# Two layers of a residual graph network on one core: row sums kept by left and right half, turned on VectorE in 32x32 blocks instead of on TensorE, tile columns in row order

## The reference

```
x = layernorm(x + adj @ (x * (u >= 0.1) / 0.9))          # layer 1
x = layernorm(x + adj @ (x @ weight) + bias)             # layer 2
```

## Time and profile before

| | us |
|---|---|
| median of 3 runs | 902.74 (902.63 to 902.84) |
| the profiled execution | 902.77 |
| its span | 901.0 |
| TensorE busy | 873.1 |
| VectorE busy | 529.6 |
| mean granted TensorE clock | 0.997 |

### The profile page before, as it was taken

One profiled execution on the slowest core, in us unless ns is written; L12 is line 12 of the kernel. 1 busy time (PEld: TensorE's weight loads), 2 busy tenths in 40 slices (PEclk: granted clock), 3 DMA queues, 4 the chain that ended last, 5 costly groups with the idle time before them and its releaser, 6 DMA issues.

```text
span 901.0 us, 13601 instructions
## 1 busy us (share of the span) xinstructions
PE 873.1 (97%) x5754; PEld 406.1 (45%) x5754; DVE 529.6 (59%) x1026; ACT 30.2 (3%) x74; POOL 25.3 (3%) x24
## 2 busy tenths in 40 slices
PE   3899999999999999999999999999999999999996
PEld 3653333333343444535354554636446456456343
DVE  6356123126145656766676667768677768768655
ACT  0100000000000000000000000000000000000011
POOL 3000000000000000000000000000000000000133
PEclk9999999999999999999999999999999999999998
DMA  9999999999999999999999999989899999999952
GB/s 373 411 416 421 420 420 420 421 421 420 420 420 422 419 420 420 420 401 410 420 420 403 413 404 380 422 352 422 359 408 419 414 417 419 420 421 419 420 242 71
DMA packets 55404, 359.60 MB, mean 399 GB/s; under 512 B 6448, under 2 KB 10544, under 8 KB 12592
## 3 DMA queue, kind: packets, MB, share of 16 engines
q1 hardware_dynamic: 55344, 358.74, 96.7%
HBM read 356.61 MB, written 2.10 MB: 398 GB/s over the span
## 4 chain that ended last, share of the span: by engine, by line
PE 92%; DMA 4%; SPq 2%; issue 1%; DVE 1%; POOLq 0%; POOL 0%; ACT 0%; DVEq 0%
PE psum L996 22%; PE psum L949 21%; PE psum L964 8%; PE psum L931 8%; PE psum L958 8%; PE psum L982 6%; PE psum L917 5%; PE psum L938 4%; PE psum L1002 4%; DMA tiles<-adj_chunks 2%; DMA tiles<-adj_t 2%; PE psum L894 1%; SPq L495 1%; PE psum L1017 1%; PE psum L1032 1%
## 5 line engine op out<-in xcount | busy, mean ns | idle before, releaser
L949 PE MATMUL psum<-tiles,stat 128*64 128x512 f32 x976 | 216.8, 593 | 0.1
L996 PE MATMUL psum<-tiles,stat 128*64 128x512 f32 x944 | 211.7, 594 | 0.0
L656 DVE TENSOR_TENSOR layer<-psum,layer 128x512 f32<-128x512 f32 (+1 forms) x143 | 98.6, 689 | 182.8 <-PE psum L996 85.6
L949 PEld LDWEIGHTS psum<-tiles,stat 128*64 128x64 f32 x976 | 69.6, 137 | 128.2 <-issue 122.5
L996 PEld LDWEIGHTS psum<-tiles,stat 128*64 128x64 f32 x944 | 66.5, 137 | 123.7 <-issue 121.4
L692 DVE TENSOR_TENSOR tiles<-tiles 128x512 f32<-128x512 f32 x90 | 62.2, 691 | 53.7 <-PE psum L940 51.7
L966 PE MATMUL psum<-tiles,stat 128*64 128x256 f32 x360 | 92.7, 380 | 0.0
L933 PE MATMUL psum<-tiles,stat 128*64 128x256 f32 x360 | 92.4, 379 | 0.0
L931 PE MATMUL psum<-tiles,stat 128*64 128x256 f32 x360 | 92.4, 379 | 0.0
L931 PEld LDWEIGHTS psum<-tiles,stat 128*64 128x64 f32 x360 | 49.3, 137 | 40.9 <-issue 20.0
L680 DVE TENSOR_TENSOR tiles<-tiles 128x512 f32<-128x512 f32 x90 | 60.6, 683 | 10.0 <-DMA tiles<-adj_t 10.0
(11 more groups left out here) (100 smaller groups left out, 849.5 us busy)
## 6 DMA issues: line engine op xcount, KB each, us to landing
tiles<-adj_t SPq DMA_DIRECT2D x306, 1024.0 KB, 13.4
tiles<-adj SPq DMA_DIRECT2D x12, 1024.0 KB, 19.2
tiles<-adj_chunks SPq DMA_DIRECT2D x12, 1024.0 KB, 20.4
tiles<-xu SPq DMA_DIRECT2D x4, 1024.0 KB, 7.9
tiles<-adj_parts SPq DMA_DIRECT2D x16, 256.0 KB, 17.7
x_res<-x SPq DMA_DIRECT2D x16, 128.0 KB, 13.9
out<-layer SPq DMA_DIRECT2D x8, 256.0 KB, 2.1
w<-weight SPq DMA_DIRECT2D x4, 16.0 KB, 9.6
```

Of the source, the lines that this page charges most:

```text
L656: return dve.tensor_tensor(out=to, in0=addend, in1=to, op=ALU.add)
L949: last = pe.matmul(sum_f[i % 2][to, :], stat[:, j * C + c, 0:D], tile[:, c], start=begun.get("f") != i and c < 2, stop=ends and c >= 2, sk ...
L996: last = pe.matmul(bank[to, :], stat[:, j * C + c, D:2 * D], tile[:, c], start=c == 0, stop=c == C - 1)
```

## The change

The sums of a row are kept differently. For each chunk c the left 256 columns of the tile are summed in PSUM partitions 0 to 63 and the right 256 in partitions 64 to 127, so every sum is complete where it stands: 8 matmuls of 256 columns in place of 4 of 512. The four transposes on TensorE and the copies on ScalarE are gone. At `row_end` VectorE adds the layer 1 part by halves, transposes 128x256 in 32x32 blocks from `halves` (row 1: straight from PSUM) to PSUM, and adds x in eight operations of 32 partitions and 128 elements each, some of them from one group of 32 partitions to another. Then it normalises as before, all of it without a filler between. `centre_weights` comes behind the norm of row 14. The part turns of block row 0 keep their transposes on TensorE.

The host now puts the columns of a tile in the order of the rows, 4p + c. So `final` reads its stationary operand with a step of 4 elements (16 bytes). Block row 0 in its first four tiles is stored by parts, and `arrived` gives them out with the part as the innermost axis: neighbouring columns lie 512 elements (2 KiB) apart there. Only `pair(0, 0)` to `pair(0, 3)` read them so.

```diff
@@ order_of_work
-            if pieces and (i > 1 or len(filler) % 2 == 0):
+            if pieces and (len(filler) == ECHO_BANKS if i > 1 else len(filler) % 2 == 0):
...
             if not turned:
                 turned = True
-                jobs.append(("turn", i - 1) if i > 1 else ("part_turn", PARTS - 1))
+                if i == 1:
+                    jobs.append(("part_turn", PARTS - 1))
...
@@ vector engine, in place of turn(k, i, c)
+            def turn(i):
+                k = turns(i) - 1
+                dve.wait_ge(s_res[i % 2], 16 * (i // 2 + 1))
+                dve.wait_ge(h_ready, k)
+                source = sum_f[i % 2] if i < EARLY else halves
+                last = dve.transpose(turned[:, 0:B // 2], source[:, 0:B // 2].rearrange("f (e p c) -> f e c p", e=2, c=C))
...
+                for side in range(2):
+                    for features in range(2):
+                        for e in range(2):
+                            at = slice((2 * side + features) * QUAD, (2 * side + features + 1) * QUAD)
+                            to = slice((2 * side + e) * QUAD, (2 * side + e + 1) * QUAD)
+                            f = slice(features * QUAD, (features + 1) * QUAD)
+                            last = dve.scalar_tensor_tensor(out=r[to, :, f], in0=t[at, e], scalar=KEPT, in1=x_rows[to, :, f],
+                                                            op0=ALU.mult, op1=ALU.add)
...
+                normalise(i, slice(0, C))
+                if EARLY <= i < NB - 2:
+                    sum_stat(i)
+                if i == NB - 2:
+                    centre_weights()
@@ vector engine, row_end
-                    dve.wait_ge(turned_ready, turns(i - 1))
                     dve.wait_ge(tile_jobs_done, done_after[job])
...
-                        dve.tensor_tensor(out=halves[of_row(i), :], in0=sum_f[i % 2][of_row(i), :],
-                                          in1=layer1_pair(i)[of_row(i), :], op=ALU.add).then_inc(half_by_dve, 1)
...
+                        own = layer1_pair(i)[of_row(i), :]
+                        step(dve.tensor_tensor(out=halves[0:D, 0:B // 2], in0=sum_f[i % 2][0:D, 0:B // 2],
+                                               in1=own[:, 0:B // 2], op=ALU.add))
+                        dve.tensor_tensor(out=halves[D:P, 0:B // 2], in0=sum_f[i % 2][D:P, 0:B // 2],
+                                          in1=own[:, B // 2:B], op=ALU.add).then_inc(half_by_dve, 1)
+                        dve.wait_ge(half_by_dve, turns(i))
+                    turn(i)
@@ tensor engine
-                    return tiles[:, slot].rearrange("p q (c b) -> p c q b", c=C)
+                    return tiles[:, slot].rearrange("p q (c b) -> p c b q", c=C)
...
                         for c in range(C):
-                            to = low if c % 2 == 0 else high
-                            last = pe.matmul(sum_f[i % 2][to, :], stat[:, j * C + c, 0:D], tile[:, c],
-                                             start=begun.get("f") != i and c < 2, stop=ends and c >= 2,
-                                             skip_group_check=True)
+                            for to, columns in (low, left), (high, right):
+                                last = pe.matmul(sum_f[i % 2][to, left], stat[:, j * C + c, 0:D], tile[:, c, columns],
+                                                 start=begun.get("f") != i and c == 0, stop=ends and c == C - 1,
+                                                 skip_group_check=True)
...
-                    for c in range(C):
-                        last = pe.transpose(turned[:, c * P:(c + 1) * P], halves[:, c * P:(c + 1) * P], ident[:, :])
-                    last.then_inc(turned_ready, 1)
...
-                            last = pe.matmul(product[n_final % 2][:, to], layer2[at, i // 2, c * P:(c + 1) * P],
+                            last = pe.matmul(product[n_final % 2][:, to], layer2[at, i // 2].rearrange("f (p c) -> f c p", c=C)[:, c],
                                              w2[at, :], start=True, stop=True)
@@ host
-    a = np.asarray(adj).reshape(NB, P, C, NB, P, C).transpose(0, 3, 4, 5, 2, 1)
+    a = np.asarray(adj).reshape(NB, P, C, NB, P, C).transpose(0, 3, 4, 5, 1, 2)
```

More of the change, by code:

```diff
@@ L34 @@
 C = 4
+QUAD = 32
 B = C * P
@@ L239, in order_of_work @@
         jobs.append(("row_end", i))
-    jobs += again[:1]
-    jobs.append(("turn", NB - 1))
-    jobs += again[1:]
+    jobs += again
     pending = None
@@ L319, in resnorm_graph_layers @@
     for job in jobs:
-        if job[0] in ("row_end", "turn"):
+        if job[0] == "row_end":
             chain_at = done_after[job]
@@ L555, in _ @@
                 elif job[0] == "row_end":
-                    i = job[1]
-                    act.wait_ge(turned_ready, turns(i - 1))
-                    act.wait_ge(tile_jobs_done, done_after[job])
-                    other = slice(D, P) if i >= EARLY and i % 2 == 0 else slice(0, D)
-                    act.activation(halves[other, :], sum_f[i % 2][other, :], ACT.Copy).then_inc(half_by_act, 1)
-                elif job[0] == "turn":
                     act.wait_ge(centred, turns(job[1]))
@@ L729, in combine, with normalise @@
                 plus(second[:, right], t_2).then_inc(combined, 1)
[L731 removed]
+            def normalise(i, c):
                 n = c.stop - c.start
[L734 removed]
                 rows, squares = r[:, c, :], sq[:, c, :]
[L736 to L747 removed]
                 centre(rows, n)
@@ L752, in turn, with turn_part @@
                                          in1=over_features(rstd[:, 0, c]), op0=ALU.mult, op1=ALU.mult).then_inc(h_ready, 1)
+            def turn_part(q):
+                rows = r[:, q:q + 1, :]
+                t = turned[:, :].rearrange("p (c f) -> p c f", c=C)[:, q:q + 1]
+                dve.wait_ge(s_res[0], 16)
+                if q:
+                    dve.wait_ge(h_ready, q)
+                dve.wait_ge(turned_ready, q + 1)
+                step(dve.scalar_tensor_tensor(out=rows, in0=t[:, :, 0:D], scalar=KEPT,
+                                              in1=x_res[:, 0].rearrange("p (c d) -> p c d", c=C)[:, q:q + 1],
+                                              op0=ALU.mult, op1=ALU.add))
+                dve.scalar_tensor_tensor(out=rows, in0=t[:, :, D:2 * D], scalar=KEPT, in1=rows,
+                                         op0=ALU.mult, op1=ALU.add).then_inc(turned_read, 1)
+                dve.wait_ge(turned_read, q + 1)
+                normalise(0, slice(q, q + 1))
@@ new lines, in turn @@
+            def turn(i):
[4 more added lines that the diff above has]
+                last = dve.transpose(turned[:, 0:B // 2], source[:, 0:B // 2].rearrange("f (e p c) -> f e c p", e=2, c=C))
+                if i < EARLY:
+                    last.then_inc(half_by_dve, 1)
+                    dve.wait_ge(half_by_dve, turns(i))
+                else:
+                    step(last)
+                t = turned[:, 0:B // 2].rearrange("p (e c f) -> p e c f", e=2, c=C)
+                x_rows = x_res[:, i % 2].rearrange("p (c d) -> p c d", c=C)
+                for side in range(2):
[6 more added lines that the diff above has]
+                                                            op0=ALU.mult, op1=ALU.add)
+                            if (side, features, e) != (1, 1, 1):
+                                last.then_inc(dve_step, 1)
+                nonlocal steps
+                steps += 7
+                dve.wait_ge(dve_step, steps)
+                last.then_inc(turned_read, 1)
+                dve.wait_ge(turned_read, k + 1)
+                normalise(i, slice(0, C))
[3 more added lines that the diff above has]
+                    centre_weights()
@@ L779, in _ @@
                 elif job[0] == "part_turn":
-                    turn(job[1], 0, slice(job[1], job[1] + 1))
+                    turn_part(job[1])
                 elif job[0] in ("chunk", "rest", "early"):
@@ L1010, in _ @@
                               start=True, stop=True).then_inc(scale_summed, 1)
-                elif kind == "turn":
-                    i = job[1]
-                    pe.wait_ge(turned_read, turns(i) - 1)
-                    pe.wait_ge(half_by_act, turns(i))
-                    pe.wait_ge(half_by_dve, turns(i))
-                    for c in range(C):
-                        last = pe.transpose(turned[:, c * P:(c + 1) * P], halves[:, c * P:(c + 1) * P], ident[:, :])
-                    last.then_inc(turned_ready, 1)
                 elif kind == "final":
@@ L1025, in _ @@
                     else:
-                        pe.wait_ge(half_by_act, turns(NB - 1))
                         pe.wait_ge(half_by_dve, turns(NB - 1))
```

30 lines of the change are left out of this document (6 added, 24 removed).

## The result

| | before | after |
|---|---|---|
| median, us | 902.76 (902.63 to 902.84) | 916.36 (916.33 to 916.44, 4 runs) |
| span of the profiled execution | 901.0 | 914.4 |
| TensorE busy | 873.1 | 885.1 |
| VectorE busy | 529.6 | 563.4 |

The changed kernel is slower by 1.5% (ratio 1.015, interval 1.0138 to 1.0162). The forecast was 897.7 us, with a range of 896 to 909: wrong by 18.7 us, and on the wrong side. TensorE should have been busy for some 8 us less. It is busy for 12 us more.

What follows compares the result with a forecast made beforehand. The prediction took TensorE and the loads as level up to about 288 us and TensorE alone as the bound after that. Its sum was 902.77 - 5.9 - 0.5 + 1.3 = 897.7 us, range 896 to 909.

Steps and rivals of the forecast that it cites:

- Strided reads on TensorE: In pair(0, 0) to pair(0, 3) and the eight finals: reading with a step costs zero; upper ends 22 and 12 us.
- Rival 1: Strided tiles of pair(0, 0) to pair(0, 3) run at half speed, 13.7 us more, ending at 908.9 us; chance 0.20.
- rival 2: Only the finals are slow, 4.4 to 8.7 us on the chain, ending at 902.1 to 906.4 us; chance 0.12.
- Transposes, -5.9 and -0.5: TensorE's turns: ten after 330 us save 0.59 us each, the fifth before it 0.5, the first four nothing.
- The level of loads and work that the prediction put at 288 us: Up to about 288 us TensorE and the loads are level, so work taken off TensorE there becomes waits for tiles.
- New order, zero within 1: Rows 1 to 3, early jobs one place later: two tile waits before 190 us, net cost zero within 1 us.
- Row sums of 256 columns, zero: First jobs on TensorE: 16 records of 256 columns replace 8 of 512, still 1.72 us a job, cost zero.
- VectorE's turn, 7.24 us: VectorE at a row's end: sums 0.90, transpose 0.45, eight additions 2.35 and norm 3.54 make the row ready after 7.24 us.
- One wait of 1.3 us after row 14, none after row 15: TensorE waits 1.3 us for VectorE's join after row 14; row 15 has 0.2 us to spare.
- First jobs, which take no bank: Rows 2 to 7: fillers are early jobs of 6.87 us or first jobs, which take no echo bank.
- Rival 3: VectorE's turn is 1.4 us longer and becomes the bound, waits after rows 8 to 15 total 6.2 us, 902.6 us; chance 0.12.
- Rival 4: The loads give way and all 15 turns count, 8.85 us saved, ending at 895.2 us; chance 0.05.

Runs made afterwards that it cites:

- run 4: TensorE alone, no graph layer, fp32 matmuls and weight loads at various column steps: a step of 2 costs 5%, of 4 a factor of 2.1.
- run 5: The kernel before with only pair(0, 0) to pair(0, 3) reading neighbouring columns 2 KiB apart: 915.57 us (1.0141).
- run 6: The kernel before with only the finals' weights read as every fourth column in place of neighbours: 910.49 us (1.0085).
- run 7: The kernel before with three of the four transposes left out of each turn: 899.24 us (0.996).
- runs_of_64: The changed kernel with columns stored so that TensorE reads runs of 64 or more, each final as 16 smaller matmuls: 899.32 us (0.9962).
- run 8: The kernel before with only the new place of the chunk and early pieces in rows 2 and 3: 904.32 us (1.002).
- runs_join_old_order: runs_of_64 with centre_weights in row 10, the first filler's join ahead of the norm, and early jobs at their old places: 899.32 us (0.9962).
- pairs_plain: The changed kernel with pair(0, 0) to pair(0, 3) reading runs of 128 neighbouring columns: 908.26 us (1.0061).
- before_new_order: The same as run 8, the kernel before with only the new job order: 904.32 us (1.002).

## Why the prediction was wrong

The step that failed is **"Strided reads on TensorE ... I take zero for both"**. The chain of reasons was that a plain stream uses every second cycle of the clock, so the reader had room. Runs 4 to 6 show no such room: a column in a line of its own takes 1056 ns a record in place of 592, at the same granted clock of 1.00. The term is 4 x 3.43 = 13.7 us on TensorE, 8.1 us of the median in this kernel (12.8 in the kernel before), and 0.98 us x 8 = 7.8 us for the finals. The prediction had both numbers, as rivals 1 and 2. They are one mechanism, and it gave them 0.20 and 0.12 as though one could come without the other. Rival 1 with slow finals adds up to 908.9 + 8.7 = 917.6 us, near the 916.4 measured; the text cut it to "up to 914", and the range to 909. Its reason was right too: behind the slow pairs no `first` job waits for a tile, and turns ahead of 288 us count as well (the seven above include those at 280 and 316 us). The lower bound of zero was picked because it was the nearest row, but no row was about the disputed thing at all.

The Trainium skill (Advanced Engine Details and Errata, "SBUF Cachelines") asks for at least two hits on a 16-byte line. Run 4 agrees: two fp32 to a line 1.05, one 2.1. The Trainium skill (SBUF — State Buffer, the note on SBUF "cachelines" in "Door 1: The DMA port swizzle") adds that one can stride for free by 4 fp32. Here one can't: a step of 4 takes 1080 ns, a step of 2 612.

The other steps:
- **Transposes, -5.9 and -0.5.** Right on where they count and small in size. From the end of row 11 to the next `raw` job before took 605.45 - 590.98 = 14.47 us, after 13.73: 0.74 us and not 0.59, as the three `pair` jobs behind the transposes took 10.45 us where 3 x 3.43 is 10.3. Over whole rows it is 0.65, since the `first` jobs give a little back (see below). The first four gave nothing in run 7. In `runs_of_64` TensorE waits for tiles once more at 319 to 324 us, 0.26 and twice 0.99 us, so the fifth turn was worth nothing there either: the `pair` that started at 329.63 us before starts at 330.58, 0.95 late. The level of loads and work that the prediction put at 288 us lies at 324 in that kernel. Run 7, with the old order, kept the gain of its fifth turn; which of the differences moves the level no run here shows.
- **New order, zero within 1.** Wrong by a little: 1.6 us (run 8). The waits came where they were foretold, and the level of 287 us did not take them back: the 0.98 us of the weight load there had cost TensorE next to nothing (run 5).
- **Row sums of 256 columns, zero.** Nearly right: four `first` jobs take 6.91 us on the chain (from 590.67), 1.727 each, where 3.5 took 6.01 before, 1.717 each. The trace has 122 such jobs (1952 / 16), so this is 1.2 us over the run that the sum did not have, at most 0.14 us in a row.
- **VectorE's turn, 7.24 us.** It is 605.44 - 597.68 = 7.76. The transpose took 0.70 with its signal and not 0.45, the eight additions 2.61 with theirs and not 2.35; the sums (0.91) and the norm (3.54) came as worked out. VectorE's additions do not overlap, as the Trainium skill (VectorE: DVE Perf Modes, "Two Vector instructions with no wait between them") has it for a change of quadrant: the eight, 0.287 us each (mean of 120), take 2.51 us.
- **One wait of 1.3 us after row 14, none after row 15.** They are 1.6 and 0.4 us in the list of waits; the half microsecond by which the turn is longer accounts for most of it. "First jobs, which take no bank" left out that two `early` fillers need four banks: hence the third wait, after row 2.
- **Rival 3**, waits after each of rows 8 to 13, has fallen: there are none. **Rival 4** too: in run 7 eleven turns count and not fifteen.

The sum of what was measured, with no term that is a difference from 916.4: 902.8 + 12.8 (pairs, run 5) + 7.8 (finals, run 6) + 2.2 (three waits for banks) - 9.8 (fifteen turns of 0.65) = 915.8, against 916.4. The new order has no term of its own here, as the slow pairs cover its waits for tiles. The terms are not quite independent, and what makes up the last 0.6 us stays open.

## What to carry to other kernels

Before the host's layout is changed, go through every operand that TensorE reads and ask how many of its neighbouring columns share 16 bytes; with fp32, one column to a line about doubles the time of a stream or of a row of weight loads (2.1 and 1.9 times), and runs of two or four cost next to nothing (1.05 and 1.0). A term that no row of the trace shows and whose bounds lie 20 us apart, on the engine that holds 92% of the chain, should be measured by itself before the sum is made, or be given its chance as one mechanism wherever it acts. What a cost is worth depends on the slack around it: the same slow pairs took 13.7 us of TensorE and were worth 12.8 us in one kernel and 8.1 in the other, by the waits for tiles that they covered.

## What the runs showed of the hardware

- VectorE's transpose of 128x256 also depends on the step of its source: 0.66 to 0.68 us from SBUF at a step of 16 bytes, 0.46 from the same place in runs of neighbours, and 0.465 from PSUM at either order of columns.

```profile
L757 DVE STREAM_TRANSPOSE psum<-halves 128x256 f32<-128x256 f32 x14 | 9.5, 677 | 0.5
```
```profile
L757 DVE STREAM_TRANSPOSE psum<-halves 128x256 f32<-128x256 f32 x14 | 6.4, 460 | 0.5
...
L757 DVE STREAM_TRANSPOSE psum<-psum 128x256 f32<-128x256 f32 x1 | 0.5, 465 | 6.2 <-PE psum L981 6.2
```

The first row is of after, the other two are of `runs_of_64`.

- A slow stream in one half of TensorE's columns does not lengthen the records of the plain one in the other half (605 ns beside 1056), but the two end together: the plain one takes 9.3 us for 16 records in place of 6.4 in run 4, and the pairs had one strided tile of two and took twice the time.
- The granted clock fell to 0.50 behind an idle time of TensorE of 4.91 us (`runs_join_old_order`, 139 to 142 us) and of 1.97 us (`pairs_plain`, 189 to 191 us). It stayed at 1.00 behind one of 1.85 us (`before_new_order`) and one of 1.76 us (`runs_of_64`), both at 187 us. How long the idle time must be these runs do not settle.
